# Ternary weights inside an attention, a new VectorE order, pieces stored early, and a delta rule on stacks of keys

## The chip, the cores and the metric

One Trainium2 chip, one core. TensorE (PE) multiplies, VectorE (DVE), ScalarE (ACT) and GpSimd (POOL) work element by element, SyncE (SP) and the others issue DMAs. The metric is the device time of one execution in microseconds (us). The kernel before took 4014.31, 4010.78 and 4014.04 us, median 4014.04.

## The reference, cut to what matters

The input X is 2 x 1024 tokens of 256 features. Eight sublayers follow one another, each added to X and each on a normalised X:

```
x += causal_attention(ln(x))       # layer 0, 16 heads of 128, bias on q, k, v, o
x += ternary_ffn(ln(x))            # "ff2"
x += delta_rule(ln(x))             # "dr3"
x += ternary_ffn(ln(x))            # "ff4", same weights as ff2
x += grouped_attention(ln(x)); x += hadamard_ffn(ln(x)); x += alibi_attention(ln(x)); x += hadamard_ffn(ln(x))
```

The weights of the ternary feed-forward are made once: per group of 64 input features, scale = mean |w| in bf16, q = round(w / scale) clipped to -1, 0, 1, and w + (q scale - w) in bf16. The layer is `h = silu(gate) * up; hn = h / rms(h); hn @ wp.T`. The delta rule splits 256 features into 16 heads of 16 and 1024 tokens into chunks of 16. k is rotated by position; for each chunk and head

```
z = kc @ W;   W = W - kc.T @ (z - vc) * (2 / 256)
```

z of all chunks is the output, which goes through a layer norm and one more projection.

## The kernel before, in words

The 2048 tokens are 16 tiles of 128 (TOK = 2048, NT = 16, QT = 8 tiles per batch, P = 128, D = 256, DC = 2 halves of the features). X stays in SBUF. The stages follow each other, each in blocks of its own with a barrier between. Products that need full f32 accuracy on the one-pass path are split into a high and a low fp32r part ("h" and "l" tiles), two or three one-pass products for one; elsewhere plain f32 is used.

`causal_attention` (L155) runs 16 heads x 2 batches = 32 halves n, each of 8 steps u (one tile of queries). A fixed list `uses` says at which step PE fills one of two PSUM banks A with which product (q, k, v, output); PE, ACT and DVE all follow it. In a half with b = 0 the next head's q and k weights are loaded and split, GpSimd makes their low parts. v's bias (1 MB) and o's bias are loaded at the begin.

`ternary_weights` (L602) runs after it, called for the gate and up weights (8 pieces of 512 columns) and the down weights (4 pieces). Per piece: ACT casts to bf16 and takes magnitudes, PE multiplies with a matrix `group` that gives the group means, DVE does seven operations (scale, two comparisons, difference, product, difference, sum), ACT puts the result in place. The next piece starts as engines come free; each piece is one chain.

`normed_swiglu` (L688) is the feed-forward, used four times: ff2 and ff4 with rms, one-part weights; ff6 and ff8 without, two-part weights. It works in 4 groups g of 4 token tiles (512 tokens), each with 8 column steps f of the hidden layer. PE does `gate_up(g, f)`, and between them the previous group's `down` in two halves, `square_sums` (rms), `turn` (transposes of the next group's normalised X into XT) and `turn_next` (transposes for the next stage, where `nxt` is given). DVE after each gate_up does hf = silu x up (L1038), the low part of h, and at a given f: `measure`/`shifted` (statistics), `normalise`, `low_turned` (low part of XT, L964; the next group's first product waits for it), `add` (y to X), and the same set for the next stage. GpSimd makes rstd and the running sum of squares. The orders are written out by hand.

`delta_rule` (L1634) has four parts: `rotary_features` (8 units of two products of 512 tokens, L1219, into kT, features by tokens), `project_tokens` for v (L1260), `turn` (32 transposes of kT into token layout, L1293), both into KV, and the main block. There, for 8 tile steps t and 4 chains q (2 batches x 2 halves of the features, 8 heads each): `product(t, p)`, p = 0..15, each two chunks, multiplies masked keys MK (a copy of the tile of keys with all rows outside one chunk of 16 zeroed, made by ACT, L1691) by [keys, values] of the tile (L1738); DVE masks the outcome to the head blocks into AB (L1778). `tile(t)` runs 8 chunk steps j: for each q a product for z (L1750, 16 columns) and one for the update U (L1755), GpSimd adds the value part to W (WB, L1721), DVE adds U (L1789). After the four chains of step j PE does products 2j and 2j + 1 of tile t + 1.

After ff8 (which has no `nxt`) a block of its own stores X with one DMA.

Of the kernel before, what the change touches and what calls it, by code (L numbers as in the profile page):

```python
# [154 lines left out]
def causal_attention(nc, name, X, XT, consts, packs, scale, tri, alibi_dram=None, out_bias=None):  # L155
# [7 lines left out]
    with Scope(nc, name) as s:  # L163
# [17 lines left out]
        if alibi:  # L181
            ramp = s.sb("ramp", [P, HEADS + SEQ])
            krow = ramp[:, HEADS:HEADS + SEQ]
            slope_row = [s.sb(f"slope_row{i}", [P, SEQ]) for i in range(2)]
        else:
            bv = s.sb("bv", [P, HEADS * DH])
            bo = s.sb("bo", [P, D])
        S = [s.ps(f"S{i}", [P, SEQ]) for i in range(2)]
# [4 lines left out]
        NCONST = 16 if alibi else 32  # L193
# [30 lines left out]
        for n in range(NHALF + 1):  # L224
# [18 lines left out]
            if r == 1:  # L243
                at += [(AT["v_high"][i], "v", n, 2 + i) for i in range(2)]
            at.sort(key=lambda x: x[0])
# [14 lines left out]
        def _(sp):  # L260
# [5 lines left out]

            def load_o(h):
                sp.dma_start(raw_o[:, :], pack_o[h]).then_inc(o_in, 16)
# [5 lines left out]
            if alibi:  # L274
                sp.dma_start(ramp[:, :], alibi_dram).then_inc(const_in, 16)
            else:
                sp.dma_start(bv[:, :], bias_v).then_inc(const_in, 16)
                sp.dma_start(bo[:, :], out_bias).then_inc(const_in, 16)
            for h in range(1, HEADS):
# [6 lines left out]
                load_o(h)  # L286

        @block.gpsimd
        def _(pool):
# [31 lines left out]

            for n in range(NHALF):
                h, b = divmod(n, 2)
                for u in range(QT):
                    if alibi:
# [9 lines left out]
        def _(pe):  # L335
# [5 lines left out]
            def use(i, what, m, which):  # L341
# [4 lines left out]
                if what in "qk":  # L346
# [87 lines left out]
        def _(act):  # L434
# [32 lines left out]

            act.wait_ge(qk_in, 16)
# [6 lines left out]
            for t in range((NHALF + 1) * QT):  # L475
# [9 lines left out]
                if not alibi and 0 <= two < NHALF * QT:  # L485
                    copy_turn(two // QT, two % QT)
                if b == 0 and u == 5 and h + 1 < HEADS:
# [12 lines left out]
        def _(dve):  # L500
# [8 lines left out]
            def take(i, what, m, which):  # L509
# [11 lines left out]
                elif what == "v" and not alibi:  # L521
                    if m == 0 and which == 0:
                        dve.wait_ge(const_in, NCONST)
                    dve.wait_ge(a_full[i % 2], i // 2 + 1)
                    pair = m // 4
                    nc.vector.tensor_tensor(V[b][:, which * 2:which * 2 + 2, :],
                                            bank[:, :].rearrange("p (t n) -> p t n", n=PAIR),
                                            bv[:, pair * PAIR:(pair + 1) * PAIR].unsqueeze(1)
                                            .broadcast_to([P, 2, PAIR]), ALU.add).then_inc(free, 1)
                elif what == "pv":  # L530
# [71 lines left out]
def ternary_weights(nc, name, consts, w_dram, dst, chunks, width):  # L602


    with Scope(nc, name) as s:
        NCOL = 512
        n = chunks * width // NCOL
        raw = s.sb("raw", [P, chunks * width])
        wb = s.sb("wb", [P, chunks * width], BF16)
        mag = s.sb("mag", [P, 2, NCOL], BF16)  # L610
        sc = s.sb("sc", [P, 2, NCOL], BF16)
        up = s.sb("up", [P, NCOL], BF16)
        dn = s.sb("dn", [P, NCOL], BF16)
        sign = s.sb("sign", [P, NCOL], BF16)
        q = s.sb("q", [P, NCOL], BF16)
        dlt = s.sb("dlt", [P, NCOL], BF16)
        out = [s.sb(f"out{i}", [P, NCOL], BF16) for i in range(2)]
        mean = [s.ps(f"mean{i}", [P, NCOL]) for i in range(2)]
        raw_in, cast_done, mag_done, mean_done, step = (s.sem(x) for x in ("raw", "cast", "mag", "mean", "step"))
        sc_done, out_done, put_done = s.sem("sc"), s.sem("out"), s.sem("put")  # L620
        block = s.block()
        dflat = dst.rearrange("p c n -> p (c n)")

        @block.sync
        def _(sp):
            sp.dma_start(raw[:, :], w_dram).then_inc(raw_in, 16)

        @block.scalar
        def _(act):
            def put(i):  # L630
                act.wait_ge(out_done, i + 1)
                nc.scalar.activation(dflat[:, i * NCOL:(i + 1) * NCOL], out[i % 2][:, :],
                                     ACT.Copy).then_inc(put_done, 1)

            act.wait_ge(raw_in, 16)
            for i in range(n):
                c = slice(i * NCOL, (i + 1) * NCOL)
                nc.scalar.activation(wb[:, c], raw[:, c], ACT.Copy).then_inc(cast_done, 1)
                act.wait_ge(cast_done, i + 1)
                if i >= 2:  # L640
                    act.wait_ge(mean_done, i - 1)
                nc.scalar.activation(mag[:, i % 2, :], wb[:, c], ACT.Abs).then_inc(mag_done, 1)
                if i >= 1:
                    put(i - 1)
            put(n - 1)

        @block.tensor
        def _(pe):
            for i in range(n):
                pe.wait_ge(mag_done, i + 1)  # L650
                if i >= 2:
                    pe.wait_ge(sc_done, i - 1)
                nc.tensor.matmul(mean[i % 2][:, :], consts["group"][:, :], mag[:, i % 2, :],
                                 start=True, stop=True).then_inc(mean_done, 1)

# [1352 lines left out]
```

## Time and profile before

| | |
|---|---|
| runs, us | 4014.31, 4010.78, 4014.04 |
| the profiled execution's own time, us | 4023.62 |
| its span, us | 4021.8 |
| busy PE / DVE / ACT / POOL, us | 3639.0 / 2523.1 / 1982.9 / 774.8 |
| attention 0 | 33 to 1009 us |
| ternary weights | 1009 to 1074 |
| ff2 | 1074 to 1228 |
| delta rule | 1229 to 1580, its tiles 1306.9 to 1537.7 |
| ff4 | 1580 to 1733 |
| grouped attention, weights of ff6, ff6 | 1734 to 2850 |
| attention 1, ff8, store | 2860 to 4021.8 |

The rows below give times from the start of the span. "PEclk" or the last columns of a window give the granted clock of TensorE as a share of 2.4 GHz; 0.50 is 1.2 GHz. In a timeline, the square bracket is the idle time before the instruction and what ended it. Timeline rows may hold several instructions of a kind (x4).

### The profile page before, as it was taken

What the parts mean: (1) busy time and instruction counts of PE and PEld (TensorE: products, weight loads), DVE (VectorE), ACT (ScalarE), POOL (GpSimd) and SP (SyncE); (2) the same over time, 40 slices, a digit from 0 to 9 for tenths busy, and PEclk for the clock granted to TensorE, in tenths of its full rate; (3) what the DMA queues carried; (4) which work ended last, traced back from release to release, by engine and by line L of the source; (5) the groups of instructions that cost most, each with busy time, mean ns of one, the idle gap of its engine ahead of it and who ended that gap; (6) DMA issues with size and microseconds to landing.
All of it is one profiled execution on the core that took longest, in us unless ns stands there. A gap on an engine that the chain in (4) does not pass through costs nothing. (4 is left out here: it accounts for less than half of the span.)

```text
span 4021.8 us, 54881 instructions
## 1 busy us (share of the span) xinstructions
PE 3639.0 (90%) x19935; PEld 2561.0 (64%) x20020; DVE 2523.1 (63%) x4927; ACT 1982.9 (49%) x4132; POOL 774.8 (19%) x844
## 2 busy tenths in 40 slices
PE   6999999999388997876999999969899999999989
PEld 5878788877265996641333333248777777777767
DVE  5656666655663664637888888725566666666643
ACT  3555555555342332414777777723355555555532
POOL 1000000000031442320000000030244444444410
PEclk9999999999698997977999999989999999999999
DMA  1000000000100000001000000010000000000000
GB/s 51 11 7 11 11 5 11 11 5 2 53 1 2 1 0 21 1 18 48 19 22 16 17 17 17 1 77 1 22 11 7 11 5 11 11 7 9 2 32 22
DMA packets 33057, 61.42 MB, mean 15 GB/s; under 512 B 7442, under 2 KB 21650, under 8 KB 30970
## 3 DMA queue, kind: packets, MB, share of 16 engines
q1 hardware_dynamic: 32810, 58.12, 4.6%
q8 instruction: 156, 2.56, 0.3%
q14 instruction: 91, 0.75, 0.1%
HBM read 48.53 MB, written 9.18 MB: 14 GB/s over the span
## 5 line engine op out<-in xcount | busy, mean ns | idle before, releaser
L1595 DVE TENSOR_REDUCE ga5m_nm<-ga5m_M 128x1 f32<-128x1024 f32 x512 | 605.9, 1220 | 128.5 <-PE ga5m_M L1498 126.6
L1583 ACT ACTIVATE ga5m_pr<-ga5m_E 128x512 f32<-128x512 f32 x1024 | 558.5, 600 | 233.7 <-PE ga5m_E L1534 216.9
L376 PE MATMUL at_A<-at_pT,at_V 128*128 128x512 f32 (+3 forms) x1536 | 519.2, 488 | 7.4 <-issue 5.0
L319 POOL TENSOR_TENSOR at_prob<-at_prob,at_slope_row 128x128 f32<-128x128 f32 (+7 forms) x256 | 369.6, 1447 | 576.6 <-DVE at_prob L570 576.4
L376 PEld LDWEIGHTS at_A<-at_pT,at_V 128*128 128x128 f32 x1536 | 283.9, 190 | 248.7 <-issue 204.3
L464 ACT ACTIVATE at_pT<-at_T 128x512 f32<-128x512 f32 (+3 forms) x768 | 347.2, 488 | 107.1 <-PE at_T L417 105.8
L1498 PE MATMUL ga5m_M<-ga5m_K,ga5m_Q 128*128 128x512 bf16 x978 | 304.3, 390 | 62.5 <-DMA ga5m_Q<-in_zrows 40.5
L417 PE MATMUL at_T<-all_ident,at_prob 128*128 128x128 f32 x2304 | 336.4, 273 | 9.0 <-ACT at_pT L464 9.0
L1534 PE MATMUL ga5m_E<-ga5m_Q,ga5m_K 128*128 128x512 bf16 x986 | 336.0, 382 | 4.1 <-ACT ga5m_pr L1583 2.6
L1534 PEld LDWEIGHTS ga5m_E<-ga5m_Q,ga5m_K 128*128 128x128 bf16 x1024 | 98.9, 97 | 302.8 <-ACT ga5m_pr L1583 221.4
L417 PEld LDWEIGHTS at_T<-all_ident,at_prob 128*128 128x128 f32 x2304 | 268.2, 140 | 31.6 <-issue 8.9
L1545 PE MATMUL ga5m_O<-ga5m_pr,ga_Vx 128*32 128x512 f32 x2048 | 272.7, 605 | 1.9 <-ACT ga5m_pr L1583 0.7
L532 DVE TENSOR_TENSOR at_aT1l<-at_A,at_aT1h 128x512 fp32r<-128x512 f32 x64 | 44.3, 692 | 327.5 <-ACT at_aT1h L444 327.5
L455 ACT ACTIVATE at_prob<-at_S,at_nbias 128x128 f32<-128x128 f32 (+7 forms) x256 | 189.4, 740 | 109.0 <-PE at_A L339 68.4
L872 ACT ACTIVATE ff_sil<-ff_gate 128x512 f32<-128x512 f32 x128 | 76.5, 597 | 312.2 <-PE ff_up L744 312.2
L455 ACT ACTIVATE at_prob<-at_prob,at_nbias 128x128 f32<-128x128 f32 (+7 forms) x256 | 199.4, 779 | 54.2 <-DVE at_nbias L560 53.3
L545 DVE SCALAR_TENSOR_TENSOR all_X<-at_A,at_rinv,all_X 128x256 f32<-128x256 f32 x512 | 212.4, 478 | 18.9 <-PE at_A L339 15.2
L1038 DVE TENSOR_TENSOR ff_hf<-ff_sil,ff_up 128x512 f32<-128x512 f32 x128 | 87.7, 685 | 213.3 <-ACT ff_sil L872 213.3
L1498 PEld LDWEIGHTS ga5m_M<-ga5m_K,ga5m_Q 128*128 128x128 bf16 x1024 | 94.1, 98 | 176.8 <-DVE ga5m_nm L1595 59.4
L444 ACT ACTIVATE at_aT1h<-at_A 128x512 fp32r<-128x512 f32 x64 | 38.3, 598 | 336.7 <-PE at_A L376 336.7
L559 DVE TENSOR_REDUCE at_nmax<-at_S 128x1 f32<-128x128 f32 (+7 forms) x256 | 194.0, 758 | 8.7
L559 DVE TENSOR_REDUCE at_nmax<-at_prob 128x1 f32<-128x128 f32 (+7 forms) x256 | 190.9, 746 | 12.5 <-POOL at_prob L319 12.5
(300 smaller groups left out, 8550.9 us busy)
## 6 DMA issues: line engine op xcount, KB each, us to landing
ga5m_Q<-ga_qs SPq DMA_DIRECT2D x96, 96.0 KB
at_raw_qk<-in_pqk SPq DMA_DIRECT2D x32, 256.0 KB, 2.8
at_raw_v<-in_pv SPq DMA_DIRECT2D x16, 256.0 KB, 3.0
at_raw_o<-in_po SPq DMA_DIRECT2D x32, 128.0 KB, 2.1
ga_qs<-ga5s_part SPq DMA_DIRECT2D x6, 512.0 KB
ga5m_K<-ga_ks SPq DMA_DIRECT2D x48, 48.0 KB
all_X<-in_x SPq DMA_DIRECT2D x1, 2048.0 KB
tq_raw<-in_gu SPq DMA_DIRECT2D x1, 2048.0 KB, 8.1
```

The lines of the kernel that those rows point to most:

```text
L319: nc.gpsimd.tensor_tensor(dst[:, 0:end], dst[:, 0:end], slope_row[n // 2 % 2][:, 0:end], ALU.add).then_inc(ramp_done, 1)
L376: mm = nc.tensor.matmul(bank[:, lo:GQ * P], V[b][:, kt, col:col + DH], pT[g][:, kt, lo:GQ * P], start=(kt == 0), stop=(kt == GQ * (g + 1) ...
L417: mm = nc.tensor.transpose(TB[(x - 1) % 2][:, (kt % 4) * P:(kt % 4 + 1) * P], prob[u % 4][:, kt * P:(kt + 1) * P], consts["ident"][:, :])
L455: nc.scalar.activation(prob[u % 4][:, 0:end], src[:, 0:end], ACT.Exp, bias=nbias[:, x:x + 1], scale=scale, accum_out=rsum[:, x:x + 1]).the ...
L464: nc.scalar.activation(pT[g][:, 4 * a:4 * a + nb, u % GQ * P:(u % GQ + 1) * P], TB[(x - 1) % 2][:, 0:nb * P].rearrange("p (k n) -> p k n", ...
L545: op = nc.vector.scalar_tensor_tensor(X[:, t, :], bank[:, j * D:(j + 1) * D], rinv[:, t:t + 1], X[:, t, :], ALU.mult, ALU.add)
L559: stepped(nc.vector.tensor_reduce(nmax[:, x:x + 1], src[:, 0:end], AX.X, ALU.max))
L1498: mm = nc.tensor.matmul(Mb[v % 2][:, lo:lo + 512], Q[n % NSLOT][:, x:x + P], K[n % NSLOT][:, lo:lo + 512], start=True, stop=True)
L1534: nc.tensor.matmul(Eb[e % 3][:, :], K[n % NSLOT][:, kt * P:(kt + 1) * P], Q[n % NSLOT][:, x:x + 512], start=True, stop=True).then_inc(s_do ...
L1545: mm = nc.tensor.matmul(Ob[32 * j:32 * j + 32, :], Vx[:, b * QT + kt, kv, :], pr[(t * NQ + j) % NR][:, :], start=(kt == 0), stop=(kt == QT ...
L1583: nc.scalar.activation(pr[e % NR][:, :], Eb[e % 3][:, :], ACT.Exp, scale=scale).then_inc(e_done, 1)
L1595: nc.vector.tensor_reduce(nm[half % 2][:, m:m + 1], Mb[v % 2][:, :], AX.X, ALU.max, negate=True).then_inc(m_free[v % 2], 1)
```

## The change

1. Ternary weights. `ternary_weights` is gone; `causal_attention` of layer 0 gets `ternary=`, the list of weights. Two pieces per head, in halves n = 2, 6, ..., 22 (12 pieces): SP loads a piece of 256 KB, ACT casts and takes magnitudes at steps 3 and 6, PE does the mean product in a bank A at steps 4 and 7, DVE does scale and two comparisons, GpSimd the five operations that are left. v's bias comes in 8 pieces of 128 KB, two buffers.
2. `normed_swiglu`, all four uses: the order on PE and DVE.
3. Store: ff8 issues 8 DMAs of 256 KB, each when its two tiles are final.
4. Delta rule: rotation, v and transposes are one block; ACT and DVE split [keys, values] of each tile into high and low fp32r parts, which SP stores to DRAM (32 stores of 256 KB). They come back as stacks: for each chunk j, KS has 48 rows (16 tokens high, high, low) of keys and KVS 48 rows (high, low, high) of [keys, values], so one one-pass product of the zero-padded tiles sums the three terms. Three loads per tile and batch on ACT's queue, three on SP's, issued when the batch's products of the tile before are done (one buffer per batch). The copies MK are gone. W and WB lie in the rotary table's room. At the main block's begin PE does 4 products of 512 columns that nobody reads, and one of 256 after each of the first tile's 16.

```diff
# causal_attention
+            def round_piece(i):                      # GpSimd
+                x, out = wb[i % 2][:, :], pieces[i][1]
+                pool.wait_ge(cut_done, 2 * i + 2)
+                nc.gpsimd.tensor_tensor(up[:, :], up[:, :], dn[:, :], ALU.subtract).then_inc(tern_step, 1)
...
+                nc.gpsimd.tensor_tensor(dn[:, :], x, up[:, :], ALU.add).then_inc(tern_step, 1)
+                nc.gpsimd.tensor_copy(out, dn[:, :]).then_inc(tern_step, 1)
...
+                elif what == "mean":                 # PE
+                    pe.wait_ge(mag_done, which + 1)
+                    mm = nc.tensor.matmul(bank[:, :], consts["group"][:, :], mag[:, :], start=True, stop=True)
...
+            def cast_piece(i):                       # ACT
+                nc.scalar.activation(wb[i % 2][:, :], raw_t[i % 2][:, :], ACT.Copy).then_inc(cast_done, 1)
+                nc.scalar.activation(mag[:, :], wb[i % 2][:, :], ACT.Abs).then_inc(mag_done, 1)
...
+                elif what == "mean":                 # DVE
+                    nc.vector.tensor_scalar(scale_of, bank[:, :], 1e-8, None, ALU.max).then_inc(free, 1)
+                    nc.vector.scalar_tensor_tensor(ups[which % 2][:, :], scale_of, 257.0 / 512.0, x,
+                                                   ALU.mult, ALU.is_lt).then_inc(cut_done, 1)
+                    nc.vector.scalar_tensor_tensor(dns[which % 2][:, :], scale_of, -257.0 / 512.0, x,
+                                                   ALU.mult, ALU.is_gt).then_inc(cut_done, 1)
# normed_swiglu, PE
                     gate_up(g, f)
-                    if nxt is not None and f == 0 and g >= 2:
-                        turn_next(g - 2)
                     if f == 1 and g:
+                        down(g - 1, 0)
                         if rms:
                             square_sums(g - 1)
-                        down(g - 1, 0)
                     if f == 2 and g:
                         down(g - 1, 1)
-                    if f == 5 and g + 1 < NG:
+                    if nxt is not None and f == 2 and g >= 2:
+                        turn_next(g - 2)
+                    if f == 4 and g + 1 < NG:
                         turn(g + 1)
-            if nxt is not None:
-                turn_next(NG - 2)
             down(NG - 1, 0)
             if rms:
                 square_sums(NG - 1)
+            if nxt is not None:
+                turn_next(NG - 2)
             down(NG - 1, 1)
# normed_swiglu, DVE, after hf and low(F - 1)
+                if f == 1:
+                    if g + 1 < NG:
+                        measure(g + 1, range(GT))
+                        shifted(g + 1)
+                    if nxt is not None and g >= 2:
+                        next_normalise(g - 2, range(GT))
+                if f == 2:
+                    if g and rms:
+                        mean_square(g - 1)
+                    if g + 1 < NG:
+                        normalise(g + 1, range(GT))
+                    if g:
+                        add(g - 1, 0)
+                        if nxt is not None:
+                            next_measure(g - 1, range(2))
+                if f == 3 and g:
+                    add(g - 1, 1)
...
-                    if f == 6:
-                        low_turned(g + 1)
+                if f in (6, 7) and g + 1 < NG:
+                    low_turned(g + 1, f - 6)
# delta_rule
+        def load_keys(engine, t, b):
+            for part, first in ((0, 0), (0, C), (1, 2 * C)):
+                engine.dma_start(KS[b][first:first + C, :, :].bitcast(F32),
+                                 kvs[part, rows_of(t, b), 0:D].rearrange("(j s) n -> s j n", s=C)
+                                 ).then_inc(k_in[b], 16)
+        def load_both(engine, t, b):
+            for part, first in ((0, 0), (1, C), (0, 2 * C)):
+                engine.dma_start(KVS[b][first:first + C, ...], kvs[part, rows_of(t, b), :]...)
...
+                    sp.wait_ge(high_done, i + 1)
+                    sp.dma_start(kvs[0, t * P:(t + 1) * P, :], kvh[:, i % NK, :, :]...)
+                    sp.wait_ge(low_done, i + 1)
+                    sp.dma_start(kvs[1, t * P:(t + 1) * P, :], kvl[:, i % NK, :, :]...)
+                    if i in (7, 9):
+                        b = (i - 7) // 2
+                        load_keys(sp, 0, b)
+                        load_both(sp, 0, b)
...
+                for t in range(1, QT):               # SP, main block
+                    for b in range(BATCH):
+                        sp.wait_ge(pp_done, (t - 1) * NP + (b + 1) * DC * PC)
+                        load_both(sp, t, b)
...
+                    if c == 0 and pair == 0:         # PE, product(t, p)
+                        pe.wait_ge(k_in[b], t * 48 + 48)
+                        pe.wait_ge(kv_in[b], t * 48 + 48)
-                        mm = nc.tensor.matmul(PP[p % 2][:, e, :, :], MK[q % 2][:, 2 * pair + e, :],
-                                              KV[:, bass.ds(t + b * QT, 1), c, :, :].rearrange("p a v n -> p (a v n)"),
+                        mm = nc.tensor.matmul(PP[p % 2][:, e, :, :], KS[b][:, 2 * pair + e, c * P:(c + 1) * P],
+                                              KVS[b][:, 2 * pair + e, :, c, :], start=True, stop=True)
...
+                for i in range(4):
+                    busy(512)
                 for p in range(NP):
                     product(0, p)
+                    busy(256)
# program
+                normed_swiglu(nc, "ff8", X, consts, [w1h, w1l], [w2h, w2l], False, (moved, 32), save=(out, saved))
```

## Rows read from the trace of the kernel before

**Rows 1.** The page's busy table: engine, busy us, share of the span, instructions.
```profile
PE 3639.0 (90%) x19935; PEld 2561.0 (64%) x20020; DVE 2523.1 (63%) x4927; ACT 1982.9 (49%) x4132; POOL 774.8 (19%) x844
```

**Rows 2.** Windows: length, busy of each engine, PEclk, DMA share, GB/s.
```profile
50.00:1005.00 955.00, 942.62 (x5317) 759.85 (x5315) 582.43 (x1333) 502.63 (x1122) 43.34 (x44) 1.00 0.03 8
1015.00:1080.00 65.00, 8.44 (x19) 2.83 (x20) 46.55 (x97) 22.15 (x37) 1.02 (x1) 0.50 0.14 52
1080.00:1235.00 155.00, 123.02 (x610) 101.08 (x609) 84.71 (x183) 61.93 (x113) 49.28 (x39) 0.86 0.01 2
1310.00:1538.00 228.00, 220.86 (x1452) 206.80 (x1451) 146.18 (x364) 67.66 (x224) 105.48 (x249) 0.95 0.00 1
```

**Rows 3.** Timeline: first load of the ternary weights, first instruction of ff2.
```profile
1009.36 0.33 SPq L626 DMA_DIRECT2D tq_raw<-in_gu  x1
...
1073.79 1.08 DVE L940 BATCH_NORM_STATS2 ff_stats<-all_X 128x6 f32<-128x256 f32 x3 [0.97 <-PEq L54]
```

**Rows 4.** Timeline of the attention's end: two one-pass products of 256 columns.
```profile
1007.15 0.28 PE L337 MATMUL at_A<-at_woh,at_aT1h 128*128 128x256 f32 x1
...
1007.27 0.28 PE L338 MATMUL at_A<-at_wol,at_aT1h 128*128 128x256 f32 x1
```

**Rows 5.** Ternary lines: line, engine, names, shapes, count, busy, mean ns, idle.
```profile
L673 DVE SCALAR_TENSOR_TENSOR tq_up<-tq_sc,tq_wb 128x512 bf16<-128x512 bf16 x6 | 4.2, 692 | 0.2
```

**Rows 6.** Waits of TensorE in ff2: waiting for, us in total, times, longest.
```profile
PE ff_turned L770 <- DVE ff_nxn L1017: 11.9, 3, 6.1
PE ff_turned L812 <- issue: 5.5, 2, 2.7
PE ff_gate L744 <- DVE ff_XT0l L964: 4.4, 2, 3.0
...
PE ff_gate L744 <- DVE ff_hf L1038: 3.6, 3, 2.9
```

**Rows 7.** Waits of TensorE in ff6.
```profile
PE ff_turned L770 <- DVE ff_nxn L1017: 2.7, 1, 2.7
...
PE ff_gate L744 <- DVE ff_XT1l L964: 0.8, 2, 0.4
```

**Rows 8.** The page's DMA issues: names, count, KB each, median us to landing.
```profile
at_raw_qk<-in_pqk SPq DMA_DIRECT2D x32, 256.0 KB, 2.8
...
out<-all_X SPq DMA_DIRECT2D x1, 2048.0 KB, 6.3
```

**Rows 9.** Timeline of the delta rule's head, PE.
```profile
1229.12 3.75 PE L1219 MATMUL dr3r_pa<-mid_XT,mid_wq 128*128 128x512 f32 x4 [0.94 <-PEq L54]
...
1262.53 17.09 PE L1260 MATMUL dr3v_acc<-mid_wv,mid_XT 128*128 128x256 f32 x64 [3.01 <-PEq L54]
...
1280.40 3.69 PE L1293 MATMUL dr3k_bank<-all_ident,dr_kT 128*128 128x128 f32 x32 [0.78 <-PEq L54]
...
1306.90 0.39 PE L1750 MATMUL dr3m_Z<-dr_kT,dr3m_W 128*128 x2 [0.97 <-DVE dr3m_AB L1778]
```

**Rows 10.** Lines of the first delta tile.
```profile
L1778 DVE TENSOR_TENSOR dr3m_AB<-dr3m_PP,dr3m_hm 128x512 f32<-128x512 f32 x16 | 11.1, 692 | 6.0 <-PE dr3m_PP L1738 6.0
...
L1789 DVE TENSOR_TENSOR dr3m_W<-dr3m_U,dr3m_WB 128x128 f32<-128x128 f32 x28 | 8.1, 289 | 2.2 <-PE dr3m_U L1755 2.0
```

**Rows 11.** Timeline of the boundary before the last delta tile.
```profile
1511.96 0.36 PE L1750 MATMUL dr3m_Z<-dr_kT,dr3m_W 128*128 128x16 f32 x2 [0.83 <-issue]
1512.03 3.33 POOL L1721 TENSOR_TENSOR dr3m_WB<-dr3m_W,dr3m_AB 128x128 f32<-128x128 f32 x8 [5.23 <-DVE dr3m_AB L1778]
...
1512.17 0.47 PE L1755 MATMUL dr3m_U<-dr3m_W,dr3m_AB 128*128 128x128 f32 x2
...
1512.62 0.47 PE L1755 MATMUL dr3m_U<-dr3m_W,dr3m_AB 128*128 128x128 f32 x2
```

**Rows 12.** Window of most of the last delta tile.
```profile
1514.50:1537.50 23.00, 22.85 (x107) 22.56 (x106) 7.95 (x28) 0.66 (x2) 11.64 (x27) 0.50 0.00 0
```

**Rows 13.** Window of narrow loads in the grouped attention.
```profile
1911.00:1920.00 9.00, 8.50 (x51) 2.96 (x52) 7.34 (x9) 6.66 (x13) 0.00 (x0) 1.00 0.34 81
```

More of the change, by code:

```diff
@@ L192, in causal_attention @@
         bias_in, const_in, bo_done = s.sem("bias_in"), s.sem("const_in"), s.sem("bo_done")
-        NCONST = 16 if alibi else 32
+        bv_in = [s.sem(f"bv_in{i}") for i in range(2)]
+        NCONST = 16
         LATE = 4 if alibi else 2
@@ L244, in causal_attention @@
                 at += [(AT["v_high"][i], "v", n, 2 + i) for i in range(2)]
+            at += [(t % QT, "mean", n, i) for i, t in enumerate(MEAN) if t // QT == n]
             at.sort(key=lambda x: x[0])
@@ L286, in _ @@
                 load_o(h)
+                if not alibi and h % 2 == 0 and h // 2 + 1 < HEADS // 2:
+                    x = index[("v", 2 * h - 3, 3)]
+                    sp.wait_ge(a_free[x % 2], x // 2 + 1)
+                    load_bv(h // 2 + 1)
+                if ternary and h % 2 == 1:
+                    for i in range(h - 1, min(h + 1, len(pieces))):
+                        if i >= 2:
+                            sp.wait_ge(cast_done, i - 1)
+                        sp.dma_start(raw_t[i % 2][:, :], pieces[i][0]).then_inc(t_in[i % 2], 16)
         @block.gpsimd
@@ L688, in normed_swiglu @@
-def normed_swiglu(nc, name, X, consts, w1, w2, rms, moved=None, nxt=None, fetch=()):
+def normed_swiglu(nc, name, X, consts, w1, w2, rms, moved=None, nxt=None, fetch=(), save=None):
     H, L = 0, 1
@@ L738, in _ @@
                     sp.dma_start(tile, source).then_inc(sem, 16)
+        if save is not None:
+            @block.sync
+            def _(sp):
+                for i in range(2 * NG):
+                    sp.wait_ge(y_out, i + 1)
+                    sp.dma_start(save[0][:, 2 * i:2 * i + 2, :], X[:, 2 * i:2 * i + 2, :]).then_inc(save[1], 16)
+                sp.wait_ge(save[1], 16 * 2 * NG)
         @block.tensor
@@ L874, in _ @@
                     high((F - 1) // FC, (F - 1) % FC)
-                if nxt is not None and f == 1 and g >= 2:
+                if nxt is not None and f == 3 and g >= 2:
                     copy_next(g - 2)
@@ L923, in _ @@
                     root(g + 1)
+                if rms and f == 2 and g:
+                    inverse(g - 1)
+                if nxt is not None and f == 5 and g:
+                    next_root(g - 1)
                 if rms:
                     gather(F)
-                    if f == 1 and g:
-                        inverse(g - 1)
-                if nxt is not None and f == 5 and g:
-                    next_root(g - 1)
             if rms:
@@ L1651, in delta_rule, with rows_of @@
-        turn(nc, name + "k", kT, lambda c, g: KV[:, 4 * g:4 * g + 4, c, 0, :], consts, False)
+        KS = [o.sb(f"KS{b}", [P, NC, D], F32R) for b in range(BATCH)]
+        KVS = [o.sb(f"KVS{b}", [P, NC, 2, DC, P], F32R) for b in range(BATCH)]
+        k_in = [o.sem(f"k_in{b}") for b in range(BATCH)]
+        kv_in = [o.sem(f"kv_in{b}") for b in range(BATCH)]
+        stored = [o.sem(f"stored{i}") for i in range(NK)]
+        def rows_of(t, b):
+            return slice((b * QT + t) * P, (b * QT + t + 1) * P)
@@ L1659, in delta_rule @@
+            W = [[room[:, (2 * q + i) * P:(2 * q + i + 1) * P] for i in range(2)] for q in range(NCH)]
+            WB = [room[:, (2 * NCH + q) * P:(2 * NCH + q + 1) * P] for q in range(NCH)]
             U = [s.ps(f"U{q}", [P, 4 * P]) for q in range(NCH)]
@@ L1898, in program @@
                 move_low(nc, kept, [w1l, w2l], moved, True)
[L1899 to L1908 removed]
+                saved = o.sem("saved")
+                normed_swiglu(nc, "ff8", X, consts, [w1h, w1l], [w2h, w2l], False, (moved, 32), save=(out, saved))
 def kernel(**inputs):
```

407 lines of the change are left out of this document (228 added, 179 removed).

## Prediction

> **What bounds the kernel now.** I read the busy table first: TensorE is busy in 90% of the span [rows 1], so a gain must come from where it stands idle, runs slow, or does work that goes away. The windows by stage show where [rows 2]. In layer 0's attention (50 to 1005 us) it is busy 942.6 of 955 us at full clock. In the two ternary stages (1015 to 1080) it is busy 8.4 of 65 us. The first rms feed-forward, ff2, has 123.0 of 155 us at a mean clock of 0.86, the delta rule's tiles 220.9 of 228. Then the waits of TensorE in each stage, and for the delta rule the lines of one tile and its boundaries.
>
> **Ternary weights.** Their loads start at 1009.36 and ff2's first instruction at 1073.79 [rows 3]: 64.4 us go. In the attention every piece adds one bf16 product of 512 columns on TensorE; 256 columns of a one-pass product are 0.12 us apart [rows 4], so 0.25, and 12 make +3.0. VectorE gets three operations a piece at 0.69 [rows 5], 24.8 in all beside 582.4 busy of 955; ScalarE gets two (some 15 us beside 502.6), GpSimd five a piece. That last form is not in the trace; eight f32 additions of 128 columns took 3.33 us [rows 11], so 1.7 for 512, 8.3 a piece and 100 in all at most, where GpSimd is busy 43 of 955. The cover is TensorE's own queue, full in 98.7% of the stage. Where VectorE's block of 2.0 us delays a softmax, TensorE waits: at nothing 0, at half a block for each of the 12 pieces 12; I take 3. v's bias in eight pieces instead of one load costs nothing: each is issued a head pair early. Result -58.4, between -61.4 and -49.
>
> **VectorE's order in the rms feed-forwards (ff2, ff4, alike).** TensorE's waits in ff2 [rows 6]: 11.9 for the next stage's normalised rows, 5.5 for square sums, 4.4 twice for the low halves of X transposed (1.4 of it before the first product, which stays), and more for hf. The new order normalises rows for the next stage two groups later, when they are long there, so the 11.9 shrink to about 3 (the last group's own chain); square sums come after a down product of 3.8 us, which hides their 2.7 each, so 5.5 becomes 0.5. The low halves now sit at f=6 and f=7, behind hf and two low operations; in a group where VectorE did other work at f=6 (3.0 us of wait) this is level, in the first it is later: 7.4 becomes 8. hf waits 0.8 more, as measure, shift and root are bunched in f=1. Sum -12.5. Less idle time also means a higher clock than 0.86 [rows 2]; I take -1.8 for it. So -14.3 a stage, -28.6; the ends are -6 each (every bunched operation waits once more) and -19 (the clock at 0.95).
>
> **The same order in ff6 and ff8.** Here TensorE waited little: 0.4 at each of three boundaries, and 2.7 once for the next stage's rows [rows 7]. The wait of 0.4 was what remained after the last low half, done at f=6. At f=7 that operation stands behind silu 0.6, hf 0.6, two lows 1.2 and itself 0.7 after TensorE's last up product of the group: 2.6 exposed in place of 0.4, for 2.2 x 3 x 2 = +13.1. A pause of 2.6 at each group may drop the clock for a stretch; the rows of ff2, with waits of 2.7 to 3.0, have a mean clock of 0.86. 0 to 10, I take +5. ff6's tail gives back 2.6.
>
> **The save.** Now one transfer of 2 MB, 6.3 us to landing; 256 KB take 2.8 [rows 8]. Only the last piece stays behind the last addition: -4 with one block less (-5 to -3).
>
> **Delta rule, its head.** Before, from the first rotation (1229.12) to the first tile product (1306.90) [rows 9]: 77.8. After: eight rotations (3.4 warm, 30.2 with the slow first), 16 tiles with v and transposes, which took 17.1 and 3.7 before [rows 9], 3.4 less as v no longer begins at the low clock after a barrier, 17.4; then the last split, its store and a block, 4.8; four idle products, 5.8 at mostly half clock, with hm's load of 2.2 beside them; 16 masked operations at 0.66 and a boundary, 11.5: 69.7. So -8 (-12 to -3). The keys' first loads start after the eighth tile and are hidden by the rest; without that cover it would be +3.
>
> **Delta rule, its tiles.** Before, one chunk step is TensorE-bound: Z and U of four chains 0.45 apart [rows 11], 1.78, and two f32 products, 1.73 by the difference: 3.51, of which eight and a boundary of 1.2 make the 29.3 a tile (230.5 less the last tile's 25.4, by seven). The new products are one-pass: 4 x 0.12 instead of 1.73, so TensorE needs 2.25. Next is VectorE: four additions at 0.28 and two masked at 0.61 (from [rows 10], which give 0.29 and 0.69 for one alone; in a row they overlap by some 0.01 and 0.08), 2.34; GpSimd needs 4 x 0.42 [rows 11] = 1.7. A step would be 2.34. ScalarE's masks were off the path. As VectorE now ends a tile late, the boundary rises from 0.8 to 1.0 to about 1.95: the last two masked operations and the lag. A tile 20.0 at full clock.
>
> Now the clock. The last tile, which has a pause of 0.83 ahead of it [rows 11] and then only Z and U, runs at 0.50, 1.2 GHz, from 1514.4 on, through 22.9 of 23.0 busy us [rows 12]. Those 23 us alone make the 0.95 of the 228 [rows 2], so the seven tiles with full products held 1.00 over pauses of 0.8 to 1.0. In the last, TensorE was not idle there; what differs from the seven tiles is thin work (a weight load for every short Z and U) without the full products between. The new tiles have thinner work than those seven everywhere, and a longer pause. I therefore take the fall to 1.2 GHz at the first boundary and no return before the end. Then a step is 4 x 0.86 (107 records, four to a Z and U, in 23.0 us) + 4 x 0.23 = 4.3, a tile 8 x 4.3 + 0.9 = 35.3. First tile 20, six at 35.3, last 27.5: 259 for 230.5 before, +29. If it held: 7 x 20 + 25.4 = 165, -65.5.
>
> The Trainium skill ("TensorE: Matmul & The Clock Gate", section "Why this matters for your kernels") asks only that pauses between bursts of matmuls stay short, and allows longer ones than 2 us; by it the clock would hold and the tiles would give the -65.5. The row of the last tile differs from that rule: it fell after 0.83.
>
> **The loads of the stacks.** Each batch and tile brings 1.13 MB in six loads to 16 partitions each, single-buffered, issued when half a tile's products are done: 12.7 us remain to hide them warm, 17 cold. For loads to 24 partitions (the queries and keys of layer 1, 1911 to 1920) the window has 81 GB/s as a mean, with gaps for the issues in it [rows 13], so at most 14.6 us; at the 2.8 us of a 256 KB load to full width [rows 8], three in a row take 8. I take them as hidden. The other bound: all packets of a queue on one of the 16 engines. 2 MB over all 16 took 6.3 us [rows 8], so the 0.75 MB of SP's three loads on one take up to 6.3 x 16 x 0.375 = 38 us.
>
> The Trainium skill ("SBUF — State Buffer", "Door 1: The DMA port swizzle") says that partitions 0 to 15 reach a quarter of the ports, 104 GB/s, and 32 to 47 the same ones. As an estimate from that page the six loads take about 13 us with both queues on those ports: hidden cold, 1 us a tile exposed warm, which leaves the sum as it is. No row has a 16-partition destination.
>
> **Sum.** -58.4 - 28.6 + 13.1 + 5 - 2.6 - 4 - 8 + 29 = -54.5. The profiled execution's span is 4021.8 and its time 4023.6; the median of the runs is 4014.0, 9.6 below it. 4023.6 - 54.5 = 3969.1; less 9.6: 3959.
>
> **Rivals.**
> (1) The clock holds at 2.4 GHz through the delta tiles. For it: seven tiles before held it over pauses, and idle products bring TensorE warm into the first tile. Against: thin work, doubled pause. Gain 94.5 more: 3865.
> (2) It falls at a later boundary, or returns within tiles. Each warm tile is worth 15.3: between 3875 and 3945, 3910 in the middle.
> (3) The other side: the stacks land late. A tile then lasts 20.0 - 12.7 = 7.3 us and one batch's load. The rest of the change gives 83.5 us; over seven tiles that is 11.9 each, so slower begins at 29.3 + 11.9 = 41.2 a tile, a load of 34 us. At the 38 us of one engine a tile takes 45.3: 7 x 16 - 83.5 = +28.5, 4043. Against: the narrow loads of 1911 us.
> (4) The pieces stall the attention by 12, ff6 and ff8 lose 10 more than taken: 3978 with the clock at 1.2 GHz.
>
> **How the numbers follow.** Forecast 0.55 (with (4) inside), (1) 0.28, (2) 0.11, (3) 0.05, 0.01 for other ends near nothing. The likeliest's own range: 3940 to 3985. To hold 8 in 10 the range needs (1) too: 3855 to 3985. A run can't tell less than 0.2%, 8 us, from no change. Faster 0.93, same 0.02, slower 0.05.
>
> **What would show it.** The ternary stages' windows gone and the attention some 6 us longer; ff2 and ff4 at 130 to 133 us for 146.6; ff6's three waits for XT low 2.6 each; the clock at 0.5 from the delta rule's first tile boundary on and tiles of 35; or 1.00 and 20 (rival 1). TensorE waiting for a DMA in the tiles means rival 3. The sum is wrong if the clock holds, or if VectorE stalls the attention by more than 12 us.

## The result

The changed kernel took 4033.73 us (median of five runs, 4028.65 to 4036.31) and the kernel before 4014.04. The ratio is 1.0045 with an interval of 1.003 to 1.0059: slower by 0.45%. The forecast was 3959, faster by 1.4%; the measured time lies outside its range on the other side. The changed kernel's profiled execution took 4031.14 us with a span of 4029.3, so the two profiles stand 7.5 us apart, and the medians 19.7: the profile of before lies 9.6 us above its median, the changed kernel's 2.6 below.

Stage by stage (from TensorE's first to last matmul of each stage, in the two profiled executions; the third column is the prediction's change):

| stage | before | forecast | after | measured change |
|---|---|---|---|---|
| attention 0 and the way to ff2's first transpose | 1040.1 | -58.4 | 994.7 | -45.4 |
| ff2 | 149.9 | -14.3 | 145.3 | -4.6 |
| delta rule, head | 77.8 | -8 | 83.0 | +5.2 |
| delta rule, tiles | 230.4 | +29 | 279.8 | +49.4 |
| ff4 | 149.8 | -14.3 | 139.4 | -10.4 |
| ff6 | 157.8 | +6.4 | 171.5 | +13.7 |
| ff8, from the attention before it to its last product | 154.6 | +9.1 | 162.3 | +7.7 |
| from the last product to the end | 7.7 | -4 | 4.4 | -3.3 |
| stages whose code is the same | 2053.7 | 0 | 2048.9 | -4.8 |

The last line is noise: over the fourteen profiles of this case these stages take 2048.9 to 2057.0 us, and the way to the grouped attention alone 100.9 to 105.4, with a stretch at 1.2 GHz of 61 to 85 us in it. ff2 isn't steady either: the same changed code took 139.3 to 146.1 us in the profiles of seven experiments below, so its -4.6 is uncertain by several us; ff4 took 139.2 to 140.2.

The windows of the changed kernel, in the order attention, ff2, the first tile's products, tiles, ff4, ff6 (columns as in [rows 2]):

```profile
50.00:1025.00 975.00, 946.90 (x5314) 761.24 (x5325) 612.47 (x1371) 515.58 (x1146) 107.66 (x100) 1.00 0.04 12
1040.00:1178.00 138.00, 114.21 (x592) 96.82 (x592) 83.44 (x181) 58.26 (x109) 50.25 (x39) 0.88 0.00 1
1249.00:1262.00 13.00, 12.93 (x68) 9.97 (x66) 10.49 (x16) 0.00 (x0) 0.00 (x0) 0.95 0.41 54
1269.00:1542.00 273.00, 265.28 (x1232) 263.30 (x1232) 144.95 (x363) 4.89 (x16) 111.55 (x248) 0.50 0.46 55
1595.00:1728.00 133.00, 109.05 (x594) 92.15 (x592) 83.45 (x181) 58.59 (x110) 50.35 (x39) 0.92 0.00 1
2694.00:2849.00 155.00, 143.74 (x804) 124.41 (x804) 72.78 (x165) 41.83 (x76) 6.29 (x6) 0.97 0.00 1
```

The fourth line is the result's largest part: 273 us with a granted clock of 0.50. In [rows 2] the same stage had 0.95. The first line shows the pieces' work beside the attention: VectorE 612 us for 582, GpSimd 108 for 43. The busy table for the answer to [rows 1]:

```profile
PE 3671.7 (91%) x19708; PEld 2613.9 (65%) x19804; DVE 2511.6 (62%) x4879; ACT 1901.0 (47%) x3872; POOL 860.0 (21%) x908
```

TensorE is busy for 33 us more although f32 products became one-pass products: in the tiles it is busy at half speed.

### The profile page after: what moved, and what is told of

Same layout as the page of the kernel before. It is cut to its first block and busy times, and to the rows that moved or that the text cites. A ratio compares the mean times of both kernels' runs of the same rounds, so it can differ in the third digit from the quotient of the medians.

```text
span 4029.3 us, 54234 instructions
## 1 busy us (share of the span) xinstructions
PE 3671.7 (91%) x19708; PEld 2613.9 (65%) x19804; DVE 2511.6 (62%) x4879; ACT 1901.0 (47%) x3872; POOL 860.0 (21%) x908
## 5 line engine op out<-in xcount | busy, mean ns | idle before, releaser
L639 DVE TENSOR_REDUCE at_nmax<-at_prob 128x1 f32<-128x128 f32 (+7 forms) x256 | 190.6, 744 | 12.6 <-POOL at_prob L353 12.6
```

The source lines that it names most:

```text
L639: stepped(nc.vector.tensor_reduce(nmax[:, x:x + 1], src[:, 0:end], AX.X, ALU.max))
```

## Experiments

All were run beside the kernel before. Where a kernel was run once, its stage times from the trace are compared, not its total. The edits are against the changed kernel.

### The delta rule alone undone

```diff
-def delta_rule(...)   # stacks, idle products
+def delta_rule(...)   # as in the kernel before
```

> The changed kernel with the delta rule of before, all else as changed. Theory: the new delta rule itself costs time, its tiles 279.8 us for 230.5 and its head 83.0 for 77.8, so without it the kernel takes 4033.7 - 54.5 = 3979, and the tiles run at full clock again. Rival: most of the loss lies in the other parts (attention +18, feed-forwards 6 and 8 +22), and the delta rule loses only because something ahead of it leaves TensorE at 1.2 GHz; then the old tiles would be slow too, above 240 us, and the time above 4000.

3963.74 us, 0.9859 of before (0.9843 to 0.9876): all the other parts together gain 1.4%, and the new delta rule costs 1.9%. That is 15 us more than the theory's sum, 11 of them because its tiles took 219.6 us here, not 230.4: the last tile ran at full clock in 14.5 us, where it took 25.4 before. The rival fell. The whole stage of tiles, and the last tile alone:

```profile
1255.00:1474.00 219.00, 212.50 (x1470) 198.43 (x1468) 147.23 (x367) 68.30 (x227) 107.43 (x255) 1.00 0.00 1
1460.00:1474.00 14.00, 14.00 (x126) 13.85 (x125) 9.04 (x31) 0.23 (x1) 13.12 (x32) 1.00 0.00 1
```

This last tile had the same pause of 0.83 us ahead of it as the one in [rows 11] and [rows 12], and the same products; there the clock fell, here it held 1.00. What the prediction took as its evidence for the fall was one outcome of two.

### Do the loads lower the clock?

In the changed kernel TensorE's waits in the tiles were (waiting for, us in total, times, longest):

```profile
PE dr3m_Z L1895 <- DVE dr3m_AB L1931: 6.3, 6, 1.1
PE dr3m_PP L1884 <- DMA dr_KS<-dr_kv: 4.4, 1, 4.4
```

and the timeline shows how the wait for the load came about: batch 0's six loads for tile 1, then batch 1's six 5.4 us behind them.

```profile
1256.18 1.27 SPq L1683 DMA_DIRECT2D dr_KVS<-dr_kv  x3
1256.18 1.34 ACTq L1677 DMA_DIRECT2D dr_KS<-dr_kv  x3
...
1261.53 1.25 SPq L1683 DMA_DIRECT2D dr_KVS<-dr_kv  x3
1261.53 1.33 ACTq L1677 DMA_DIRECT2D dr_KS<-dr_kv  x3
...
1268.88 1.22 PE L1884 MATMUL dr3m_PP<-dr_KVS,dr_KS 128*128 128x256 f32 x4 [4.37 <-DMA dr_KS<-dr_kv]
```

The six loads of each batch are issued "when half a tile's products are done". In the steady state this leaves half a tile. For tile 1 it doesn't: tile 0's products stand in the head, one after the other, and tile 1's first product follows them after one step of four chains. TensorE was ready for it at 1264.5, 8.3 us after batch 0's loads were issued; they landed by 1268.8, after 12.6. (In the later tiles a batch's loads took 11.2 to 12.2 us.) The clock fell at 1267.4, within that wait of 4.37 us.

```diff
-                        sp.wait_ge(pp_done, (t - 1) * NP + (b + 1) * DC * PC)
-                        load_both(sp, t, b)
...
-                        act.wait_ge(pp_done, t * NP + (b + 1) * DC * PC)
-                        load_keys(act, t + 1, b)
```

> The loads of the stacks for tiles 1 to 7 are left out, the products use tile 0's stacks again (so z is not the reference's). Theory D: the clock fell because TensorE waited 4.4 us for the keys of tile 1 in the first step of tile 0; without that wait tile 0 takes about 20 us at 2.4 GHz. Theory P, the prediction's: thin work and a boundary pause make it fall anyway, at the first boundary, so tiles 1 to 6 take 34 to 36 us and all tiles 255 to 262. If D alone is right, the clock holds and the tiles take 165 to 175.

Both theories were right in their part. Tile 0 took 19.67 us at 2.4 GHz; then came the first boundary, a pause of 1.33 us that ended at 1282.28, and the clock fell at 1284.1. The tiles took 259.3:

```profile
1262.00:1283.00 21.00, 19.13 (x168) 18.86 (x167) 17.61 (x49) 0.66 (x2) 14.38 (x34) 1.00 0.01 2
1285.00:1522.00 237.00, 230.25 (x1070) 228.27 (x1068) 125.36 (x316) 4.61 (x14) 98.09 (x218) 0.50 0.00 0
```

So the prediction's step on the clock holds (it had 20 and 259), and the wait for tile 1's loads adds 20.5 us, nearly all of it by making tile 0 slow too: 38.6 us for 19.7.

### Idle products in the waits

```diff
+                            if first and j == 0:       # tile 0 only
+                                for x in range(10):
+                                    idle(1 - slot)     # 512 columns, identity x kT, into the free Z bank
                             product(t + 1, 2 * j)
                             product(t + 1, 2 * j + 1)
+                    if following:
+                        pe.wait_ge(z_out, t + 2)
+                        for x in range(4):
+                            idle(1 - slot)
```

PE's tile loop is unrolled for it.

> Idle products of 512 columns fill TensorE's waits: ten in the first step of tile 0 ahead of the products that wait for a load, four at each tile's end. If pauses between thin work cost the clock, it now holds at 2.4 GHz: tiles of 20 to 22 us, all of them 170 to 185 for 279.8, the kernel at 3925 to 3940. Rival: the thin work alone cannot hold the clock, it falls within a tile in spite of the filling, and the time stays above 4000.

3926.56 us, 0.9772 of before (0.9753 to 0.9792). The tiles took 173.7 us at a clock of 1.00: tile 0 30.2, six of 21.5, the last 14.5.

```profile
1259.00:1434.00 175.00, 173.91 (x1327) 155.60 (x1327) 130.39 (x369) 5.27 (x16) 109.95 (x256) 1.00 0.80 92
```

With the waits filled, the thin work held 2.4 GHz in stretches of 18.1 us between groups of idle products, and of 14.5 us in the last tile. The 107 us between this and the changed kernel are what filling two kinds of pauses is worth here, one of 4.4 us and seven of 1.0 to 1.2, less the idle products' own time. Two things changed at once, though: the pauses went, and wide products came in their place. No run fills a pause with thin work, so which of the two holds the clock isn't shown.

### Only at the boundaries

```diff
-                                for x in range(10):    # none in tile 0's first step
```

> The changed kernel with the four idle products at each tile's end alone, none ahead of the products that wait for tile 1's loads. Theory: the wait of 4.4 us in tile 0's first step lowers the clock as before, and four idle products at a boundary do not bring it back between thin work, so the tiles take 278 to 295, as slow as the change or slower. Rival: a burst of idle products at a boundary (3.4 us at 1.2 GHz) lifts the clock again; then it is back after the first or second boundary and the tiles take 185 to 215.

My theory fell. The clock went down in tile 0 as in the changed kernel, and the idle products of the first boundary brought it back for good, 2.0 us after the first of them began (at 1300.7): tile 0 took 41.6 us, the next six 21.5 each, all 185.1, the kernel 3934.76. The 30 us of thin work ahead of them, without a pause, had not.

```profile
1268.00:1300.00 32.00, 32.00 (x146) 31.36 (x147) 18.41 (x44) 0.00 (x0) 10.92 (x25) 0.50 0.56 66
1301.00:1447.00 146.00, 145.69 (x1142) 132.83 (x1140) 112.72 (x320) 4.54 (x14) 95.39 (x222) 1.00 0.77 88
```

The four idle products themselves (two passes each):

```profile
1298.69 4.62 PE L1914 MATMUL dr3m_Z<-dr_kT,all_ident 128*128 128x512 f32 x8
```

Four idle products are a longer stretch than I took: one of 512 f32 columns takes 0.85 us at full clock (ten of them 8.75 in the trace), so four would take 6.8 at half clock, not 3.4. These took 4.6, as the clock rose among them.

### The idle products of the change

```diff
-                for i in range(4):
-                    busy(512)
                 for p in range(NP):
                     product(0, p)
-                    busy(256)
```

> The changed kernel without the idle products at the delta rule's begin. Theory: in the changed kernel they buy little, as the clock falls in tile 0's first step anyway: the head is 2 to 4 us shorter, the tiles the same 280 within 2, the kernel 0 to 4 us faster. Rival: they hold the clock for the head; without them the head's masked operations wait for slow products and the head is no shorter, the kernel 2 to 6 us slower.

The head took 82.2 us for 83.0, the tiles 278.5 for 279.8: as the theory in sign, with less gain than it had. Without the idle products TensorE stays at 1.2 GHz from 1231.5, ahead of the first tile's products, to the end of the tiles:

```profile
1247.00:1263.00 16.00, 10.83 (x32) 7.89 (x32) 10.69 (x20) 0.00 (x0) 0.00 (x0) 0.50 0.45 60
```

The change's idle products bring TensorE warm into tile 0, where the load wait ends it; in the changed kernel they buy nothing that these two profiles show.

### No stacks at all

```diff
-                        wait_stored(sp, 0, b)
-                        load_keys(sp, 0, b)
-                        load_both(sp, 0, b)
```

and as in the kernel without reloads.

> No stack is loaded at all, the products multiply the zeroed tiles (z is not the reference's); the stores stay. Theory: the head's end (17.4 us from the last transpose to the first idle product) is made by the first tile's loads, which share the queue and the DMA engines with the stores; without them the stores land as the prediction had it, the gap is 5 to 7 us and the head 70 to 73 for 83.0. Rival: the 32 stores alone are too much for the queue, and the gap stays above 14. The tiles as without reloads: 255 to 262, the clock falling at the first boundary.

Idle time before the main block's first idle product, in the changed kernel and then in this one:

```profile
1244.85 6.39 PE L1907 MATMUL dr3m_Z<-dr_kT,all_ident 128*128 128x512 f32 x8 [17.36 <-PEq L54]
```

```profile
1232.53 5.51 PE L1902 MATMUL dr3m_Z<-dr_kT,all_ident 128*128 128x512 f32 x8 [5.42 <-PEq L54]
```

17.4 us became 5.4, and the head took 70.2 (the prediction had 69.7). The head's loss is the loads'. The tiles took 259.6 us, and the clock fell 1.5 us after the end of the first boundary's pause of 1.33, much as in the kernel without reloads. Data rate and busy share of the DMA engines in the changed kernel from 1205 to 1245, 1 us a slice:

```profile
DMA  0000079999999999999999999999999999999950
GB/s 0 0 0 0 0 287 412 397 414 404 325 143 171 123 100 123 133 104 131 133 381 397 368 169 152 107 113 147 119 145 186 358 406 410 404 412 399 373 207 0
```

Stores to DRAM run at about 400 GB/s; when the loads to 16 partitions come in (from 1216 and from 1228 on), the engines stay fully busy at 100 to 180, and the last stores come out behind them, after 1236. That loads are slow as such is ruled out by [rows 2]: the ternary weights, loaded to full width, moved 52 GB/s at a busy share of 0.14, some 370 GB/s of busy time. No run loads the stacks' bytes to more partitions, so the narrow destination is the likely cause and not a tested one. The Trainium skill ("SBUF — State Buffer", "Door 1: The DMA port swizzle") gives 104 GB/s for such a destination; the trace agrees in size, with 100 to 133 GB/s in the slices from 1218 to 1224.

### Half of the first loads behind the stores

```diff
-                    if i in (7, 9):
-                        b = (i - 7) // 2
+                    if i in (7, NT - 1):
+                        b = 0 if i == 7 else 1
```

on top of the sum below.

> The sum of the mended parts with the first stacks of batch 1 loaded after the last store instead of after the tenth tile. Theory: the stores' end waits for the loads that share the queue and the engines; with half of these behind the stores the gap ahead of the main block falls from 17.4 to 10 to 12 us, batch 1's stacks land before its first product needs them, and the kernel takes 3875 to 3878 for 3882.4. Rival: the loads only move and TensorE waits for them in the head's second half; then the head stays at 81 to 84 and the time at 3880 to 3885, or above if the clock falls there.

3876.45 us, 0.9652 of before (0.9636 to 0.9669), against 3882.41 (0.9668). The gap fell to 9.5 us and the head to 76.2; this and the two versions at the end, which lie within its interval, are the fastest measured, and it beats the kernel before by 3.5% and the changed one by 3.9%.

```profile
1219.89 6.33 PE L1919 MATMUL dr3m_Z<-dr_kT,all_ident 128*128 128x512 f32 x8 [9.47 <-PEq L54]
```

### GpSimd after both cuts

```diff
-                pool.wait_ge(cut_done, 2 * i + 2)
+                pool.wait_ge(cut_done, 4 * (i // 2) + 4)
```

> GpSimd begins a pair of pieces only when VectorE has made the cuts of both. Theory: VectorE's second comparison takes 1.65 us for 0.69 because GpSimd works on bf16 tiles beside it; without it the attention's six waits of 1.86 us fall to about 0.7 and the attention takes 981 us for 988.1. Rival: the operation is long for another reason (where its operands lie) or TensorE waits for the block of three operations whatever their length, and the attention stays at 986 to 988.

The attention took 981.1 us for 988.1. In the changed kernel, VectorE and GpSimd:

```profile
133.04 0.68 DVE L604 TENSOR_SCALAR at_sc<-at_A 128x512 bf16<-128x512 f32 x1
...
133.76 0.93 DVE L606 SCALAR_TENSOR_TENSOR at_up<-at_sc,at_wb 128x512 bf16<-128x512 bf16 x1
...
134.22 1.49 POOL L368 TENSOR_TENSOR at_dn<-at_wb,at_up 128x512 bf16<-128x512 bf16 x1
...
134.61 1.65 DVE L608 SCALAR_TENSOR_TENSOR at_dn<-at_sc,at_wb 128x512 bf16<-128x512 bf16 x1
```

and with the edit, the same VectorE operations:

```profile
132.87 0.68 DVE L604 TENSOR_SCALAR at_sc<-at_A 128x512 bf16<-128x512 f32 x1
133.58 0.69 DVE L606 SCALAR_TENSOR_TENSOR at_up<-at_sc,at_wb 128x512 bf16<-128x512 bf16 x1
134.19 0.69 DVE L608 SCALAR_TENSOR_TENSOR at_dn<-at_sc,at_wb 128x512 bf16<-128x512 bf16 x1
```

TensorE's waits in the attention, first of the changed kernel, then with the edit:

```profile
PE at_A L390 <- DVE all_X L625: 11.0, 6, 1.9
PE at_A L432 <- DVE all_X L625: 4.5, 6, 0.8
```

```profile
PE at_A L432 <- DVE all_X L625: 4.5, 6, 0.8
PE at_A L390 <- DVE all_X L625: 4.0, 6, 0.7
```

The same comparison takes 1.65 us or 0.69, as GpSimd works beside it or not. What stays, 4.5 and 4.0, I put down to the block of three operations; no run takes it apart.

### The low halves at f=6

```diff
-                if f in (6, 7) and g + 1 < NG:
-                    low_turned(g + 1, f - 6)
+                if f == 6 and g + 1 < NG:
+                    low_turned(g + 1, 0)
+                    low_turned(g + 1, 1)
...
-                    if f == 4 and g + 1 < NG:
+                    if f == (4 if rms else 5) and g + 1 < NG:
                         turn(g + 1)
```

> Feed-forwards: both low halves of the transposed X again at f=6, and the transposes of the next group after f=5 again in the two without rms. Theory: TensorE's waits of 2.61 us at each of the three group boundaries of ff6 and ff8 fall to 0.4 and the 3.26 us ahead of the last transposes of ff6 go, so ff6 takes 159 to 162 for 171.5 and ff8 154 to 156 for 162.3; in ff2 and ff4 the boundaries of 3.2, 4.2 and 3.2 fall to 0.4 to 1.5 and each takes 5 to 9 us less. Rival: at f=6 VectorE is late for another reason (hf waits for silu) and the waits only change their name; then each stage stays within 2 us.

ff6 156.2, ff8 155.1, ff2 137.1 and ff4 133.1 us. TensorE's waits in ff6 of the changed kernel, and with the edit:

```profile
PE ff_gate L747 <- DVE ff_XT1l L966: 5.2, 2, 2.6
...
PE ff_turned L760 <- issue: 3.3, 1, 3.3
...
PE ff_gate L747 <- DVE ff_XT0l L966: 2.6, 1, 2.6
```

```profile
PE ff_gate L747 <- DVE ff_XT1l L966: 0.8, 2, 0.4
PE ff_turned L760 <- issue: 0.5, 1, 0.5
PE ff_gate L747 <- DVE ff_XT0l L966: 0.4, 1, 0.4
```

In the rms stages the boundaries of 3.2, 4.2 and 3.2 us became 2.0, 2.2 and 2.0, not the 0.4 to 1.5 expected: why they don't fall further isn't shown. The edit undoes two things at once, so what each is worth in ff6 isn't separated. For ff2, 137.1 stands against the 139.3 to 146.1 of the seven profiles with the changed order; for ff4, 133.1 against 139.2 to 140.2.

### The sum, and less filling

Idle products, GpSimd after both cuts and low halves at f=6 together:

> Together: idle products in the waits of the delta tiles, GpSimd after both cuts, low halves at f=6. If the three are independent the gains add to the 3926.6 of the filled kernel: attention -7, ff2 and ff4 -5 to -9 each, ff6 -10, ff8 -7, so 3880 to 3895. Rival: denser stages lose elsewhere what they gain (clock, SBUF port), and it stays above 3905.

3882.41 us, 0.9668 of before (0.9651 to 0.9684), as the theory had it. The attention took 981.0, the tiles 173.7, ff2 and ff4 138.8 and 131.4, ff6 and ff8 156.0 and 154.1.

On top of the kernel with batch 1's stacks late, five idle products for ten and two for four:

> As the kernel with batch 1's stacks late, but five idle products instead of ten in tile 0's first step and two instead of four at each tile's end. An idle product of 512 columns took 0.85 us in the trace, so ten cover 8.7 us of a wait of 4.4, and four cover 3.4 us of a pause of 1.3 to 1.9. Theory: the surplus goes: tile 0 takes 25.8 for 30.1, the others 19.8 for 21.5, all tiles 158 to 162 for 173.7, the kernel 3861 to 3865 for 3876.4, the clock at 2.4 GHz. Rival: with less filling the clock falls at a boundary and the time goes up, by 15 us for each slow tile.

3873.65 us, 0.9640 (0.9619 to 0.9661), no measurable gain on 3876.45. The tiles took 166.8 us, tiles 1 to 6 19.8 to 20.8 each, and they now wait for loads:

```profile
PE dr3m_PP L1885 <- DMA dr_KS<-dr_kv: 2.5, 4, 1.4
```

Tile 0 took 30.9 for the 25.8 expected, as the clock fell in it: at 1261.7, after the wait of 1.41 us for a load, and back at 1271.9, 0.6 us after tile 0's idle products began.

```profile
1262.00:1271.00 9.00, 9.00 (x44) 9.00 (x43) 5.19 (x13) 0.00 (x0) 3.07 (x7) 0.50 0.45 61
...
1271.26 2.22 PE L1915 MATMUL dr3m_Z<-dr_kT,all_ident 128*128 128x512 f32 x4
```

One idle product a boundary:

> The same with one idle product at each tile's end. Theory: 0.85 us leaves a pause of 0.4 to 1.1 us; the tiles keep 19.7 us, as the unfilled warm tile took, and the clock holds as it held over pauses of 0.8 to 1.0 in the kernel before: the kernel within 3 us of the one with two. Rival: the stretch between is too thin and the clock falls at the first boundary: tiles of 35.6, the kernel above 3940.

3875.98 us, 0.9652 (0.9635 to 0.967). The tiles took 165.9 us. The clock held over all seven boundaries, with a pause of 0.4 us or less left at each, and over two load waits of 0.91 and 0.93 us. It fell once, at 1321.7, after a load wait of 1.83 us, and came back at 1332.0, 0.6 us after that tile's idle product began; that tile took 26.2.

```profile
1322.00:1331.00 9.00, 9.00 (x44) 9.00 (x44) 5.11 (x13) 0.00 (x0) 3.13 (x8) 0.50 0.55 57
1333.00:1352.00 19.00, 18.78 (x160) 17.95 (x159) 17.24 (x48) 0.66 (x2) 13.25 (x32) 1.00 1.02 122
```

```profile
1331.40 1.30 PE L1915 MATMUL dr3m_Z<-dr_kT,all_ident 128*128 128x512 f32 x2
```

The surplus filling is gone, but at some 20 us a tile the stacks have no time left to land in: the DMA share in the window from 1333 is 1.02.

## Why the prediction was wrong

The step that failed is the one on the loads of the stacks, "I take them as hidden", which put them at nothing. The time a load takes was about right (11.2 to 12.6 us, where the prediction had 8 to 14.6); the time that hides it was not. "12.7 us remain to hide them warm" doesn't hold for tile 1, which had 8.3, and nothing hid the first stacks, which I let be "hidden by the rest" of the head. These two places cost 12.8 us (head 83.0 against 70.2 without loads) and 20.5 us (tiles 279.8 against 259.3). For the tiles in the loop 12.7 is just enough: filled tiles of 21.5 us never waited for a load, tiles of some 20 us waited 2.5 to 4.0 in all. Rival (3) had the right place with a price from one engine serving a queue; the loads in fact kept all 16 engines busy, at 100 to 180 GB/s.

- Ternary weights: the 3.0 us of products are right. "I take 3" for the stalls was too little: 15.5 us were waited (11.0 and 4.5), of which 7.0 were GpSimd stretching a VectorE operation. The upper end of 12 was too low as well, as I put nothing on two engines working on SBUF together, though the trace of before had 0.69 only for operations that ran without GpSimd.
- ff2 and ff4: -4.6 and -10.4 for -14.3. The boundaries were 3.2, 4.2 and 3.2, 10.6 in all, for "7.4 becomes 8"; the next stage's rows took 4.8 for "about 3"; a wait of 2.3 for normalised rows ahead of the second transposes and 2.1 for the low part of h were not in the sum.
- ff6 and ff8: "2.6 exposed in place of 0.4" is right to 0.01 us. Missing was a wait of 3.3 ahead of ff6's transposes, which the change moved a step earlier; it fell to 0.5 when both parts were moved back.
- Head: right to 0.5 us without the loads, in sum; its terms weren't measured one by one.
- Tiles: the fall of the clock at the first boundary, 19.7 at full clock (20.0), 35.6 at half (35.3) and 259 in sum are as forecast, where the loads are left out; the pause of a warm boundary was 1.3 us, not 1.95. The 20.0 doesn't follow from its own terms: eight steps of 2.34 and 1.95 make 20.7, and the 19.7 measured is eight of 2.29 and 1.33. The fall itself came in both kernels without reloads, so that step holds, but its evidence was partly luck: the last tile of before held the clock in the kernel with the old delta rule. "Thin work" was named as the reason beside the pause, and it isn't enough: with the pauses filled, the same thin work held 2.4 GHz.
- Save: -3.3 for -4.

In sum: loads and tiles 34, attention 13, feed-forwards 19, save 1: 67 us more than forecast, less 5 of noise in the unchanged stages, is the 62 between the profiles. Most of the other 12.7 of the 74.7 between forecast and median is the profiles' places beside their medians (9.6 above, 2.6 below); the forecast took off 9.6 as if the changed kernel's profile lay there too. My range took the ends of the costs singly; nearly all of them came out on the same side.

The rule of the Trainium skill ("TensorE: Matmul & The Clock Gate", section "Why this matters for your kernels"), by which pauses longer than 2 us would do no harm, is not what the runs show here: without loads the clock fell after a boundary of 1.3 us and stayed down for 240.

## What to carry to other kernels

When loads are issued "when the last use is done", check the first and the last iteration by themselves: the time that hides them in the loop may not exist there. Before a product is made cheaper, ask what keeps the clock up once TensorE has pauses: here the tiles with one-pass products were slower by 49 us (29 of them with no load in their way), and faster by 57 once idle products filled the pauses. Loads into 16 partitions were slow here; their price was DMA time, and the stores beside them paid it too. And don't lean on the clock of one stretch in one profile: the same last tile took 25.4 us in one execution and 14.5 in another.

## What the runs showed of the hardware

- In the delta tiles the granted clock fell to 1.2 GHz after pauses of TensorE of 1.33 (twice), 1.41 and 1.83 us and in or after load waits of 3.8 to 4.5. It held over pauses of 0.33 to 0.98, except once: it fell after 0.83 ahead of the last tile of before, and held over the same pause in the kernel with the old delta rule.
- Once down, it stayed down through 240 to 280 us of thin work with pauses of 1.0 to 1.2 us. Each of the three times that it came back within the tiles, idle products of 512 f32 columns had begun 0.6, 0.6 and 2.0 us before.
- A VectorE comparison on 128x512 bf16 tiles took 0.69 us alone and 1.65 beside a GpSimd addition on bf16 tiles, which itself took 1.49 for 1.16.
- Loads of stacks to 16 partitions kept the 16 DMA engines busy at 100 to 180 GB/s, stores from 128 partitions at some 400.
- GpSimd's two-input bf16 operations of 512 columns took 1.16 us, its f32 ones 1.29.
